# Wide cross attention of a two-layer decoder: context rows padded to 96, values made in lanes, Pool normalises, batches in one pipeline

## What is computed

```python
x = x + _L1_xattn_ref(_layernorm(x, axis=-1), ctx_1024, ...)

xn = _layernorm(x, ln_gamma, ln_beta)          # a second norm
q = (xn @ w_q).reshape(B, SQ, 16, 64)
k, v = jnp.split(context @ w_kv, 2, axis=-1)   # each (B, 77, 16, 64)
scores = jnp.einsum('bqhd,bkhd->bhqk', q * SCALE, k)
attn = jax.nn.softmax(scores, axis=-1)
out = jnp.einsum('bhqk,bkhd->bqhd', attn, v).reshape(B, SQ, 1024)
return (out @ w_out + b_out) * jnp.tanh(gate[0])
```

## Time and profile before

| what | us |
|---|---|
| median of 3 runs | 1975.33 |
| lowest and highest run | 1973.99, 1980.15 |
| the profiled execution | 1974.62 |
| its span, first to last instruction | 1972.8 |
| stage 5, start to last add to x | 1202 to 1709.6 |
| of it the fold | 1206.2 to 1215 |

### The profile page before, as it was taken

The page is one execution under the profiler, slowest core; times in us unless marked ns, Lnnn a source line. Parts: engine busy times, 40 slices in busy tenths (PEclk is TensorE's granted clock), DMA queues, the critical chain, the costliest instruction groups (busy, mean ns, idle before and its releaser), DMA issues. The chain is left out here.

```text
span 1972.8 us, 34150 instructions
## 1 busy us (share of the span) xinstructions
PE 1641.7 (83%) x12375; PEld 1137.2 (58%) x12375; DVE 1139.3 (58%) x2830; ACT 757.5 (38%) x1319; POOL 530.8 (27%) x520
## 2 busy tenths in 40 slices
PE   3989999977999699999599995888898888749880
PEld 2555555545666577776266664566676666535570
DVE  1556666645766455654388985665556655573231
ACT  1212222215666334333277763444444444302240
POOL 0344444443212011110377772000000000045006
PEclk9999999998999899999699998999999999859995
DMA  3600000000000000000000000000000000003213
GB/s 101 189 4 5 6 5 6 5 1 11 6 9 8 1 1 0 0 0 1 22 2 2 2 2 4 4 0 3 3 3 3 0 3 4 1 0 102 70 59 91
DMA packets 55322, 36.53 MB, mean 19 GB/s; under 512 B 14137, under 2 KB 50742, under 8 KB 55094
## 3 DMA queue, kind: packets, MB, share of 16 engines
q1 hardware_dynamic: 53174, 30.95, 5.6%
q0 software_dynamic: 2048, 4.20, 0.8%
HBM read 23.59 MB, written 11.55 MB: 18 GB/s over the span
## 5 line engine op out<-in xcount | busy, mean ns | idle before, releaser
L135 POOL TENSOR_TENSOR s_ln_variance<-s_ln_moments,ln_eps 128x4 f32<-128x4 f32 x40 | 8.0, 200 | 635.4 <-DVE s_ln_moments L129 635.4
L955 ACT COPY s_pT<-bank 77x512 f32<-77x512 f32 (+1 forms) x256 | 139.9, 585 | 94.4 <-PE bank L1132 94.3
L1132 PE MATMUL bank<-ident,s_p 128*77 128x128 f32 (+1 forms) x1024 | 146.7, 282 | 23.1 <-ACT s_pT L955 13.0
L1132 PEld LDWEIGHTS bank<-ident,s_p 128*77 128x77 f32 (+1 forms) x1024 | 113.9, 146 | 59.4 <-issue 36.2
L1767 PEld LDWEIGHTS bank<-s_v,s_pT 77*128 77x128 f32 x1024 | 123.6, 192 | 34.5 <-issue 18.1
L1288 ACT ACTIVATE s_hT<-bank,w_s_b 128x512 f32<-128x512 f32 x128 | 88.0, 687 | 138.9 <-PE bank L1401 137.4
L1645 ACT COPY s_v<-bank 77x512 f32<-77x512 f32 x128 | 74.5, 582 | 166.9 <-PE bank L1740 166.9
L1740 PE MATMUL bank<-s_vo,s_ctxT 128*77 128x512 f32 x256 | 132.1, 597 | 5.4 <-ACT s_v L1645 5.4
L1409 PEld LDWEIGHTS bank<-w_s_w2T,s_hT 128*128 128x128 f32 x1024 | 122.5, 192 | 23.9 <-issue 16.3
L868 POOL TENSOR_TENSOR s_p<-s_p,s_peak 128x1024 f32<-128x1024 f32 x64 | 120.1, 1897 | 55.2 <-DVE s_peak L1015 55.2
L1767 PE MATMUL bank<-s_v,s_pT 77*128 77x128 f32 x1024 | 125.3, 276 | 5.1 <-DVE x_all L1692 5.1
(11 more groups left out here) (251 smaller groups left out, 3459.1 us busy)
## 6 DMA issues: line engine op xcount, KB each, us to landing
sorted_tokens<-s_rows SPq DMA_DIRECT2D x1, 3072.0 KB, 12.3
routed_tokens<-s_xnT SPq DMA_DIRECT2D x12, 256.0 KB, 2.3
s_ctxT<-ctxT SPq DMA_DIRECT2D x16, 154.0 KB, 2.2
w_s_gateup<-s_gateup SPq DMA_DIRECT2D x1, 2048.0 KB
out<-x_all SPq DMA_DIRECT2D x8, 256.0 KB, 2.6
lam_scratch<-s_soft SPq DMA_DIRECT2D x8, 128.0 KB, 1.7
s_lam<-lam_scratch SPq DMA_DIRECT2D x64, 16.0 KB, 1.7
w_s_w1T<-s_w1T SPq DMA_DIRECT2D x1, 1024.0 KB
```

Source lines behind the costliest of these rows:

```text
L955: nc.scalar.copy(pT[0:keys, b % 2, 4 * q:4 * q + 4, :].rearrange("m h t -> m (h t)"), bank[0:keys, flip_bank("p", b, q), :]).then_inc(drai ...
L1132: last = nc.tensor.transpose(bank[0:keys, into, j * T:(j + 1) * T], p[:, b % 2, 4 * q + j, :], core.ident[:, :])
```

## The change

Every batch of stage 5 is one step of a pipeline over all 32 batches, with no hardware loop. Step b does scores of b, values and flips of b-1, weighing of b-2; four key matmuls of the next group are spread over each step.

- The context is kept in three buffers with 96 rows a batch, of which 19 are zero. The weights `p` are 96 wide a head, their last 19 columns zero. Four heads are 384 columns, which are three tiles of 128: 12 flips and 12 weighing matmuls a batch.
- Values are made in that layout: `lane_pieces` gives for each quad of heads eight pieces (tile, lane, lanes, head, row) of 64 or 32 lanes, each a matmul of 128 columns.
- Keys, values, flips of p and of xn all go through a ring of three banks (4 to 6), in an order fixed in `place`, and ACT copies all of them.
- Pool multiplies by the inverse sums (`share`) in place of DVE.
- The values' buffers lie on weights that are no longer read (`folded_away`).
- Semaphores are plain ones; Pool zeroes `ctx` and `p` during the fold.

```diff
+MP = 96
+QUAD = 4
+TILES5 = H * MP // P
+PER_QUAD = TILES5 // QUAD
...
+def lane_pieces():
+
+    pieces = []
+    for head in range(QUAD):
+        row = 0
+        while row < MP:
+            tile, lane = divmod(head * MP + row, P)
+            lanes = 64 if lane % 64 == 0 and MP - row >= 64 else 32
+            pieces.append((tile, lane, lanes, head, row))
+            row += lanes
+    return sorted(pieces)
...
-        ctxT = sbuf("s5_ctxT", [P, GM])
-        kT = sbuf("s5_kT", [P, H, GM])
-        v = sbuf("s5_v", [P, G, H * D])
...
+        ctx = sbuf("s5_ctx", [P, 3, G, MP])
+        kT = sbuf("s5_kT", [P, 2, H, GM])
+        p = sbuf("s5_p", [P, 2, H, MP])
...
+        pT = sbuf("s5_pT", [P, 2, TILES5, T])
+        folded_away = (w.s5_wvT, w.s5_wo, w.s1_wq, w.s1_wk)
+
+        def values(b, q):
+
+            return folded_away[b % 2 * 2 + q // 2][:, q % 2 * PER_QUAD:(q % 2 + 1) * PER_QUAD, :]
+
+        sem = core.plain_semaphore
...
+        SCORE5, RING, RINGS, OUT = 0, 4, 3, 7
...
+        take("xn", 0)
+        for h in range(H):
+            take("k", 0, h)
+        for step in range(BATCH + 1):
+            for q in range(QUAD):
+                if step:
+                    take("v", step - 1, q)
+            for q in range(QUAD):
+                if step:
+                    take("p", step - 1, q)
+                if heads_in(step):
+                    take("k", step // G + 1, heads_in(step)[q])
+            if step % G == G - 1 and step // G + 1 < GROUPS:
+                take("xn", step // G + 1)
+
+        def ring_bank(*user):
+            return RING + place[user] % RINGS
...
+            @block.gpsimd
+            def _(pool):
+                nc.gpsimd.memset(ctx[:, :, :, :], 0.0).then_inc(cleared, 1)
+                nc.gpsimd.memset(p[:, :, :, :], 0.0).then_inc(cleared, 1)
...
+                sp.wait_ge(cleared, 2)
+                for g in range(GROUPS):
+                    if g >= 3:
+                        sp.wait_ge(filled, place["v", G * (g - 2) - 1, QUAD - 1] + 1)
+                    sp.dma_start(ctx[:, g % 3, :, 0:M],
...
+                def share(b, u):
+                    pool.wait_ge(inverse_ready, 2 * b + u + 1)
+                    heads = slice(HU * u, HU * (u + 1))
+                    part = p[:, b % 2, heads, 0:M]
+                    nc.gpsimd.tensor_tensor(part, part, inverse[:, b % 2, heads].unsqueeze(2).to_broadcast([P, HU, M]),
+                                            ALU.mult).then_inc(share_ready, 1)
...
+                for step in range(BATCH + 1):
+                    for q in range(QUAD):
+                        if step:
+                            keep_values(step - 1, q)
+                    for q in range(QUAD):
+                        if q % 2 == 0 and step < BATCH:
+                            exp_of(step, q // 2)
+                        if step:
+                            keep_pT(step - 1, q)
+                        if heads_in(step):
+                            keep_key(step // G + 1, heads_in(step)[q])
+                    if step % G == G - 1 and step // G + 1 < GROUPS:
+                        keep_xnT(step // G + 1)
...
+                for step in range(BATCH + 2):
+                    g = step // G + 1
+                    if step < BATCH:
+                        soften(step, 0)
+                        soften(step, 1)
...
+                    if step < BATCH:
+                        total_of(step, 0)
+                        total_of(step, 1)
+                    if step >= 2:
+                        add_to_x(step - 2)
...
+                def fill(*user):
+
+                    if place[user] >= RINGS:
+                        pe.wait_ge(drained, place[user] - RINGS + 1)
+                    return ring_bank(*user)
...
+                def values_of(b, q):
+                    into, g = fill("v", b, q), b // G
+                    for tile, lane, lanes, head, row in lane_pieces():
+                        last = nc.tensor.matmul(bank[lane:lane + lanes, into, tile * D:(tile + 1) * D],
+                                                ctx[:, g % 3, b % G, row:row + lanes], vo[:, QUAD * q + head, :],
+                                                start=True, stop=True, tile_position=(0, lane))
+                    last.then_inc(filled, 1)
...
+                def flip_p(b, q):
+                    pe.wait_ge(share_ready, 2 * b + q // 2 + 1)
+                    into = fill("p", b, q)
+                    flat = p[:, b % 2, QUAD * q:QUAD * (q + 1), :].rearrange("p h m -> p (h m)")
+                    for j in range(PER_QUAD):
+                        last = nc.tensor.transpose(bank[:, into, j * T:(j + 1) * T], flat[:, j * P:(j + 1) * P],
                                                    core.ident[:, :])
...
+                for step in range(BATCH + 2):
+                    if step < BATCH:
+                        scores_of(step)
+                    if 1 <= step <= BATCH:
+                        for q in range(QUAD):
+                            values_of(step - 1, q)
+                    for q in range(QUAD):
+                        if 1 <= step <= BATCH:
+                            flip_p(step - 1, q)
+                        if heads_in(step):
+                            key_of(step // G + 1, heads_in(step)[q])
+                    if step % G == G - 1 and step // G + 1 < GROUPS:
+                        flip_xn(step // G + 1)
+                    if step >= 2:
+                        weigh(step - 2)
```

More of the change, by code:

```diff
@@ new lines, in stage5 @@
+        cleared = sem("s5_cleared")
+        ctx_landed = [sem(f"s5_ctx_landed{k}") for k in range(3)]
+        stats_ready = sem("s5_stats_ready")
+        moments_ready = sem("s5_moments_ready")
+        variance_ready = sem("s5_variance_ready")
+        rstd_ready = sem("s5_rstd_ready")
+        xn_ready = sem("s5_xn_ready")
+        xn2_ready = sem("s5_xn2_ready")
+        filled = sem("s5_filled")
+        drained = sem("s5_drained")
+        scored = sem("s5_scored")
+        peak_ready = sem("s5_peak_ready")
@@ new lines, in stage5, with take, heads_in @@
+        place = {}
+        def take(*user):
+            place[user] = len(place)
+        def heads_in(step):
+            return range(step % G * QUAD, step % G * QUAD + QUAD) if step // G + 1 < GROUPS and step < BATCH else ()
+        take("xn", 0)
[12 more added lines that the diff above has]
+                take("xn", step // G + 1)
@@ L1630, in _ @@
+                rstd_of(0, 0)
+                rstd_of(0, 1)
+                bias_x(0)
+                for b in range(BATCH):
+                    g = b // G + 1
+                    share(b, 0)
+                    share(b, 1)
+                    if g < GROUPS:
+                        if b % G == 0:
+                            rstd_of(g, 0)
+                        if b % G == 1:
+                            rstd_of(g, 1)
+                            bias_x(g)
             @block.scalar
             def _(act):
[L1632 to L1658, removed]
@@ L1695, in turn @@
[L1695 to L1714, removed]
+                def moments_of(g, which, source):
+                    k = 2 * g + which
+                    for n in range(G):
+                        last = nc.vector.bn_stats(stats[:, n, :], source(n))
+                    last.then_inc(stats_ready, 1)
+                    dve.wait_ge(stats_ready, k + 1)
+                    core.hold_vector()
+                    for n in range(G):
+                        last = nc.vector.bn_aggr(moments[:, which, n, :], stats[:, n, :])
+                    last.then_inc(moments_ready, 1)
@@ L1789, in _, with flip_xn @@
-                flip_norm(0)
-                keys_of(0, range(H))
-                turns(pe, turn)
+                def fill(*user):
+                    if place[user] >= RINGS:
+                        pe.wait_ge(drained, place[user] - RINGS + 1)
+                    return ring_bank(*user)
+                def flip_xn(g):
+                    into = fill("xn", g)
+                    pe.wait_ge(xn2_ready, g + 1)
+                    for n in range(G):
+                        last = nc.tensor.transpose(bank[:, into, n * T:(n + 1) * T], xn2[:, n, :], core.ident[:, :])
+                    last.then_inc(filled, 1)
@@ new lines, in key_of @@
+                def key_of(g, h):
+                    into = fill("k", g, h)
+                    pe.wait_ge(ctx_landed[g % 3], (g // 3 + 1) * 16)
+                    nc.tensor.matmul(bank[:, into, 0:GM].rearrange("p (n m) -> p n m", m=M), kq[:, h, :],
+                                     ctx[:, g % 3, :, 0:M], start=True, stop=True).then_inc(filled, 1)
+                def values_of(b, q):
[4 more added lines that the diff above has]
+                                                start=True, stop=True, tile_position=(0, lane))
+                    last.then_inc(filled, 1)
@@ new lines, in scores_of @@
+                def scores_of(b):
```

(20 more changed lines are left out.)

241 lines of the change are left out of this document (122 added, 119 removed).

## The result

The changed kernel takes 1986.94 us (median of 5 runs, 1984.92 to 1988.82) against 1976.96 (5 runs of the kernel before, 1973.99 to 1980.15). The ratio is 1.0054, with a 95% interval of 1.0037 to 1.0071. The profiled span grew from 1972.8 to 1986.6 us, 13.8 us where the medians differ by 10.0: the profiled execution of before lies 2.3 us under its median of 5, that of after 1.4 us over its own. All of the 13.8 lies in stage 5: its main part now goes from 1235.09 us, first scores, to 1723.0, last add, 487.9 us instead of 474.1.

What follows compares the result with a forecast made beforehand. PE was taken to bound stage 5, 13.0 of 14.8 us a batch. The main part summed to 473.7 us against 474.1 (-0.4), the start to -1.4 and +1: -0.8 in all, 1974.5 us, range 1872 to 1998.

Steps and rivals of the forecast that it cites:

- A: Stage 5's values: each change of tile width drains PE, values 5.78 us a batch; 1974.5 us in all; chance 0.50.
- B: Rival on stage 5's values: no drain between 64 and 32 lanes, values 2.8 us a batch; 1878 us; chance 0.18.
- C: Rival on stage 5's values: only colliding columns wait, values 4.1 us a batch; 1920 us; chance 0.12.
- Every change of width drains: Stage 5's values: each switch between tile widths costs some 0.09 us in which nothing streams.
- D: Rival on stage 5's values: two 64-column tiles don't run side by side; 2018 us, with drains 2080; chance 0.12.
- The size of a run: Stage 5's values: pieces of one width in a row take 0.34 us, 17 times a batch: 5.78 us, +2.36.
- Scores at 2.07: Stage 5's four score matmuls a batch keep their matmuls and columns, 2.07 us of PE time.
- Flips and keys, 4.40 in the ring's grip: Stage 5 steps with keys: 3.4 us without waits, plus a 1.0 us stall for banks that ScalarE drains in order.
- Rival E: Stage 5's ring doesn't stall because ScalarE hands banks back sooner: -28 us, 1946 us; chance 0.08.
- Flips -0.44, weighing -0.90: Stage 5, PE time a batch: both go from 16 to 12, saving 0.44 and 0.90 us.
- Pool's share: Stage 5: Pool's multiply by inverse sums takes 1.2 us, twice a batch, and hides, being wanted a step later.
- The start: Start of stage 5: DVE's wait falls from 4.22 to 2.82 us (-1.4); memsets delay its scaling (+1).

Runs made afterwards that it cites:

- the last order of exps with one width: Changed kernel with all value pieces 32 lanes wide, first exp ahead of all values copies, second ahead of the third: ratio 0.9452 to the kernel before.

## Why the prediction was wrong

The forecast was 1974.5 us, with 0.53 for faster. The likeliest case, A, was the one that happened, and its mechanism was right; three of its terms were too small, and three tenths of the chance had gone to B and C, against which every change of tile in the rows spoke.

- **Every change of width drains: right.** The runs with one width and with grouped pieces show it. Rivals B and C (no drain, or only for colliding columns) would have made a quad 0.65 or 1.0 us; it is 1.5. D is out too: 64-lane tiles overlap.
- **The size of a run: the step that failed.** "A run takes 0.20 to the first record, 0.11 + 0.03 to the second: 0.34" came out as 0.356, and values as 6.05 us a batch instead of 5.78. 0.27 x 32 batches = 8.6 us. A run of 32 lanes was sized right, at 0.342. A run of 64 lanes takes 0.369, and the sum gave it the same 0.34, from rows that have no tile of 64 lanes beside another width.
- **Scores at 2.07:** they take 2.17, because the drain ahead of the first values shows there (2.08 in the run without the padding, where values use no tiles of 64 or 32 lanes). +0.1, 3 us over the stage.
- **Flips and keys, 4.40 in the ring's grip: right in kind and place** (waits ahead of the second and fourth key), 4.54 measured, +0.14 x 27 = 4 us. "Exp ahead of a p copy" as its cause is shown: with both exps moved the phase takes 3.45, the 3.4 of the sum without waits. Rival E was out.
- The step was 15.43 instead of 14.94, and 0.49 x 26 is 12.7 of the 14.2 us by which the main part missed its sum (487.9 against 473.7). Beside that, the four steps without keys take 12.97 us or more each instead of 12.54 (+1.8), and a norm flip adds 0.43 us instead of 0.55 (-0.8).
- **Flips -0.44, weighing -0.90: right** (2.67 a step against 2.69). Keys as before. Pool's share 1.23 us, hidden: right, as PE never waits for Pool in the steady steps. **The start** was to be -1.4 + 1; DVE's wait fell by 1.6 and its scaling took 0.6 more. The first scores came at 1235.09 instead of 1235.6, in one execution of each.
- **The sign.** The forecast was off by 12.4 us, or 0.6%, and it had the wrong direction: 0.8 us less, where 10.0 us more was measured. The measured time lies inside case A's own range of 1960 to 1992 us. Its -0.8 us was what was left of gains of 1.34 and 1.8 us a batch (flips and weighing, the old turn's waits) and losses of 2.36 and 1.0 (values, the ring), some 100 us on either side. Such a remainder could carry no direction: the text itself gave case A 11 us for 0.02 us a run, and the measured run is 0.016 over the forecast. Of the 0.53 for faster, 0.38 came from B, C and E.

## What to carry to other kernels

Here tiles of one size ran side by side, four at 0.029 us a record where one alone takes 0.11, and a change of size in the stream cost about 0.14 us; with a change at every second piece, a quad also needs four rounds instead of three. Before cutting a shape into mixed tiles, count the changes. Group the pieces by size (3.35 us for the same 64 records), or pay for more pieces of one size (96 records in 2.76 us against 64 in 6.05). When one engine hands banks back in a fixed order, put its work that nobody waits for soon where it is idle, not ahead of a copy that frees a bank. Parts of a change should be timed alone: here the pipeline's gain of 1.8%, and the 5.5% of the last order of exps with one width, were hidden behind the widths and the order of small matmuls.

## What the runs showed of the hardware

- Tiles 64 and 32 columns wide that touch different columns still don't overlap: between them weight loads stand for 0.17 to 0.20 us, and a run two records deep takes 0.369 us (64) or 0.342 us (32) where it takes 0.22 in a stream of one width. The Trainium skill ("TensorEngine Tiling (Array Packing)", Key Properties) says that a change of mode drains TensorE, and the trace agrees; the price is the runs'.
- Pieces of one width overlap fully when neighbours in the stream have different lanes (0.029 us a record), and only in part when three in a row want the same lanes (0.047 us a record); the starts fit one waiting piece being passed.
- Memsets of Pool's beside VectorE stretched a scaling from 0.75 to 1.35 us and the next one from 0.28 to 2.75 us. That one ended 0.08 us after the memset, and so did the PSUM evictions queued behind it, the first of them 1.36 us long against 0.28 for the later ones. Pool's own memset took 3.20 us for 3072 floats, against 2.7 by the 0.87 ns each of the earlier trace rows. The stage's start was no later for it: in the two profiled executions its first scores came 0.5 us sooner than before.
